# Attention in a four-phase kernel: projections at other steps, rows of maxima issued by SyncE, and an opening with buffers of its own

## The reference

```python
x = x + attention(layernorm(x))      # 4 sequences of 1024 tokens, 256 wide, 16 heads of 16, causal
x = x + moe(layernorm(x))            # one of 4 experts per token
x = x + (layernorm(x) + mamba2(layernorm(x)))
x = x + moe(layernorm(x))

def attention(x):                    # W + B A of the sequence's LoRA adapter, for Q, K, V and O
    Q, K, V = multilora(x, q), multilora(x, k), multilora(x, v)
    Q, K = rope(Q), rope(K)
    scores = where(causal, Q K^T / sqrt(16), -inf)
    return multilora(softmax(scores) V, o)
```

## Time and profile before

| | |
|---|---|
| three runs | 2194.78 us (median), 2182.81 to 2199.73 |
| the profiled execution | 2185.0 us, span 2183.1 us |
| mean granted clock of PE | 0.901 |
| busy: PE, DVE, ACT, POOL | 83%, 55%, 38%, 33% |
| DRAM read, written | 102.52 MB, 45.48 MB |

### The profile page before, as it was taken

One profiled execution on the slowest core, in us unless ns is written; L12 is line 12 of the kernel. 1 busy time (PEld: TensorE's weight loads), 2 busy tenths in 40 slices (PEclk: granted clock), 3 DMA queues, 4 the chain that ended last, 5 costly groups with the idle time before them and its releaser, 6 DMA issues. The chain is left out here.

```text
span 2183.1 us, 30159 instructions
## 1 busy us (share of the span) xinstructions
PE 1819.3 (83%) x9520; PEld 1212.1 (56%) x9520; DVE 1191.3 (55%) x2979; ACT 822.7 (38%) x1705; POOL 725.6 (33%) x922
## 2 busy tenths in 40 slices
PE   5368889889888864899999658989898938999997
PEld 3133334434433322788888535747484727888886
DVE  4466676666666508543443356665656685443442
ACT  2036655656665624111111035554646441111111
POOL 2335464464462312222222124333242312222221
PEclk9569989989988855999999969999999978999999
DMA  5522333332442108000000230100101080000000
GB/s 160 174 89 90 119 126 95 122 125 77 134 135 87 39 16 313 22 24 28 26 25 26 70 111 15 43 36 1 78 1 78 1 309 22 26 24 30 25 24 9
DMA packets 90179, 161.23 MB, mean 74 GB/s; under 512 B 23080, under 2 KB 50476, under 8 KB 88880
## 3 DMA queue, kind: packets, MB, share of 16 engines
q1 hardware_dynamic: 71504, 107.39, 14.7%
q0 software_dynamic: 17984, 50.62, 7.2%
q10 hardware_dynamic: 544, 1.31, 0.2%
HBM read 102.52 MB, written 45.48 MB: 68 GB/s over the span
## 5 line engine op out<-in xcount | busy, mean ns | idle before, releaser
L690 ACT ACTIVATE a_probs<-a_ps_e 128x512 f32<-128x512 f32 (+3 forms) x768 | 336.0, 491 | 204.1 <-PE a_ps_e L854 200.9
L438 DVE CUSTOM_DVE_ANT_0 a_ps_m<-a_ps_m,a_causal 128x512 f32<-128x512 f32 (+3 forms) x512 | 239.4, 517 | 97.5 <-PE a_ps_m L841 96.4
L1433 PE MATMUL g_ps_y<-g_w_d,x_res 128*128 x1120 | 253.2, 379 | 2.8 <-DVE x_res L1203 2.8
L854 PE MATMUL a_ps_e<-a_q_st,a_k_st 64*128 64x512 f32 (+3 forms) x768 | 187.9, 480 | 76.4 <-ACT a_probs L690 48.5
L854 PEld LDWEIGHTS a_ps_e<-a_q_st,a_k_st 64*128 64x128 f32 x768 | 79.6, 201 | 289.8 <-ACT a_probs L690 200.5
L1433 PEld LDWEIGHTS g_ps_y<-g_w_d,x_res 128*128 128x128 f32 x1120 | 212.3, 190 | 34.6 <-issue 3.2
L442 DVE TENSOR_REDUCE a_peak<-a_ps_m 128x1 f32<-128x512 f32 x256 | 164.8, 686 | 94.8 <-PE a_ps_m L841 94.1
L841 PE MATMUL a_ps_m<-a_k_st,a_q_st 64*128 64x512 f32 (+3 forms) x768 | 152.7, 399 | 68.8 <-DMA a_k_st<-a_scr_k 28.0
L1323 ACT COPY x_res<-g_ps_h 128x512 f32<-128x512 f32 x70 | 41.1, 587 | 439.2 <-PE g_ps_h L1441 439.2
L576 POOL TENSOR_SCALAR_AFFINE_SELECT a_probs<-a_probs 128x256 f32<-128x256 f32 x256 | 103.9, 408 | 284.1 <-ACT a_probs L690 283.8
L1170 DVE BATCH_NORM_STATS2 g_xe_stats<-x_res 128x6 f32<-128x256 f32 x70 | 29.9, 426 | 295.6 <-DMA x_res<-g_x_rows,g_token_i 295.6
(11 more groups left out here) (272 smaller groups left out, 3664.5 us busy)
## 6 DMA issues: line engine op xcount, KB each, us to landing
a_q_st<-a_scr_q POOLq DMA_DIRECT2D x32, 512.0 KB, 4.0
a_k_st<-a_scr_k POOLq DMA_DIRECT2D x32, 512.0 KB, 4.8
m_spread_acs<-m_acs_rows SPq DMA_DIRECT2D x8, 2048.0 KB, 9.7
a_scr_q<-a_high SPq DMA_DIRECT2D x36, 256.0 KB
a_scr_k<-a_high SPq DMA_DIRECT2D x36, 256.0 KB
a_swapped<-a_raw SPq DMA_DIRECT2D x64, 128.0 KB, 2.0
g_w_gu<-L_ffn_Wg SPq DMA_DIRECT2D x8, 1024.0 KB, 9.8
g_w_gu<-L_ffn_Wu SPq DMA_DIRECT2D x8, 1024.0 KB, 12.4
```

The lines of the kernel that those rows point to most:

```text
L438: nc.vector.tensor_tensor_reduce(ps_m[:, bank, 0:w], ps_m[:, bank, 0:w], causal[:, 512 - w:], 1.0, MASKED, ALU.add, ALU.max, peak[:, p % 2 ...
L690: nc.scalar.activation(probs[:, N % RING, r, q0:], ps_e[:, (2 * N + r) % HEAD_BANKS, q0:], ACT.Exp, scale=DH ** -0.5).then_inc(exp_done, 1)
L854: nc.tensor.matmul(ps_e[:, (2 * N + r) % HEAD_BANKS, q0:], k_st[rows(r), p % BUFS, j * P:(j + 1) * P], q_st[rows(r), p % BUFS, 512 * c + q ...
L1433: last = nc.tensor.matmul(ps_y[:, 0:D], hid_t[:, f * P:(f + 1) * P], w_d[:, bass.ds(e, 1), f].rearrange("p a d -> p (a d)"), start=(f == 0 ...
```

## The change

Six things are changed, all in the attention.

1. The projections of Q, K and of the values move from steps 3, 5, 7, 9 to steps 2, 8, 14, 20. The copies, turns, rounding and storing that follow move with them, into the next unit for parts 2 and 3. The low-rank product for the output moves from step 13 to 11.
2. `put_rows` moves from POOL to SP. ACT's copy before it writes rounded values.
3. Parts 2 and 3 of block 0 get buffers of their own (`first_high`, `first_low`, in memory of `a_probs` that is unused until the first exponentials), so ACT no longer waits for a landing before it rounds them.
4. For block 0, SP writes parts 0 and 2 and ACT writes parts 1 and 3.
5. SP loads x of sequences 1 to 3 only when pair 0 has landed.
6. The row statistics of sequence 1 are taken between chunks 22 and 42, those of sequences 2 and 3 in units 1 and 5, one tile behind a step's maxima.

```diff
-    LORA_AT, XT_AT, OUT_AT, QK_AT, V_AT, LORA_O_AT = (1, 4, 9), (6, 7, 12, 13), (15, 17, 19, 21), (3, 5, 7, 9), (3, 5, 7, 9), 13
+    LORA_AT, XT_AT, OUT_AT, QK_AT, V_AT, LORA_O_AT = (1, 4, 9), (6, 7, 12, 13), (15, 17, 19, 21), (2, 8, 14, 20), (2, 8, 14, 20), 11
...
+        def parts(blk, i):
+            if blk == 0 and i >= 2:
+                return first_high[:, i % 2], first_low[:, i % 2]
+            return high[:, i % 2], low[:, i % 2]
+
+        def keep(eng, blk, i):
+            eng.wait_ge(low_ready, 4 * blk + i + 1)
+            n, half = i % 2, i // 2
+            to = scr[n][blk % 2, :, :, :, half * 512:(half + 1) * 512]
+            hi, lo = parts(blk, i)
+            for c, part in enumerate(((hi, hi, None, lo), (hi, lo, None, hi))[n]):
+                if part is not None:
+                    eng.dma_start(to[:, c], part).then_inc(scr_out[i % 2], 16)
...
+            def put_rows(p):
+
+                sp.wait_ge(piece_act, ACT_NO["max", p] + 1)
+                for r in range(2):
+                    sp.dma_start(q_st[64 * r + 32:64 * r + 33, p % BUFS, :].bitcast(F32), less_t[r * T:(r + 1) * T, p % 2, :]).then_inc(rows_in[p % BUFS], 16)
...
-            for i in range(4):
-                keep(0, i)
+            for i in (0, 2):
+                keep(sp, 0, i)
+            sp.wait_ge(pair_in[0], 32)
             for b in range(1, BATCH):
                 sp.dma_start(X[:, b * T:(b + 1) * T], x[:, b * T:(b + 1) * T]).then_inc(x_in[b], 16)
-            for i in range(4):
+            for i in range(3):
                 swap(1, i)
-            for i in range(4):
-                keep(1, i)
+            keep(sp, 1, 0)
+            put_rows(0)
+            swap(1, 3)
+            for i in (1, 2):
+                keep(sp, 1, i)
+            put_rows(1)
+            keep(sp, 1, 3)
...
+                    for p in MAX_AT.get(U * CORE + n, []):
+                        put_rows(p)
...
-                    if g % 2 == 1 and more and n in (4, 6, 8, 11):
-                        swap(2 * b + 2 + g // 2, (4, 6, 8, 11).index(n))
-                    if g % 2 == 1 and more and n in (17, 19):
-                        keep(2 * b + 2 + g // 2, (17, 19).index(n))
-                    if g % 2 == 0 and U >= 2 and (U - 1) // GROUPS + 1 < BATCH and n in (3, 6):
-                        keep((U - 1) // GROUPS * 2 + 2 + (U - 1) % GROUPS // 2, 2 + (3, 6).index(n))
+                    if g % 2 == 1 and more and n in (3, 9, 15, 21):
+                        swap(2 * b + 2 + g // 2, (3, 9, 15, 21).index(n))
+                    if g % 2 == 1 and more and n in (14, 20):
+                        keep(sp, 2 * b + 2 + g // 2, (14, 20).index(n))
+                    if g % 2 == 0 and U >= 2 and (U - 1) // GROUPS + 1 < BATCH and n in (3, 9):
+                        keep(sp, (U - 1) // GROUPS * 2 + 2 + (U - 1) % GROUPS // 2, 2 + (3, 9).index(n))
...
-            for b in range(1, BATCH):
-                dve.wait_ge(x_in[b], 16)
-                moments(b)
-            maxima(0, CUTS[0])
+            for k in range(0, CUTS[0], 2):
+                maxima(k, k + 2)
+                if k in range(22, 22 + 2 * T, 2):
+                    row_moments(1, (k - 22) // 2)
+                if k == 42:
+                    moments(1)
...
+                    if g == 1 and b + 2 < BATCH and n in range(10, 10 + T):
+                        row_moments(b + 2, n - 10)
+                    if g == 1 and b + 2 < BATCH and n == 20:
+                        moments(b + 2)
...
-            ROPE_AT = {6: (0, 0), 7: (0, 1), 8: (0, 2), 9: (1, 0), 10: (1, 1), 11: (1, 2), 12: (2, 0), 13: (2, 1),
-                       14: (2, 2), 15: (0, 3), 17: (1, 3), 19: (3, 0), 21: (3, 1), 23: (3, 2)}
+            ROPE_AT = {5: (0, 0), 6: (0, 1), 7: (0, 2), 11: (1, 0), 12: (0, 3), 13: (1, 1), 14: (1, 2), 17: (2, 0),
+                       18: (1, 3), 19: (2, 1), 20: (2, 2), 23: (3, 0)}
+            ROPE_THEN = {0: (3, 1), 1: (2, 3), 2: (3, 2), 7: (3, 3)}
...
-                    for p in MAX_AT.get(U * CORE + n - 1, []):
-                        put_rows(p)
...
-                if blk >= 1 or i >= 2:
+                if blk >= 1:
                     act.wait_ge(scr_out[i % 2], 48 * (2 * blk + i // 2))
...
                 if e == ("v", 0, 0):
                     for i in range(4):
                         round_high(0, i)
+                    for i in (1, 3):
+                        keep(act, 0, i)
```

56 lines of the change are left out of this document (26 added, 30 removed).

## The result

The changed kernel took 2212.44 us (median of 11 runs), the kernel before 2189.49 beside it. The ratio is 1.0082, with a 95% interval of 1.0054 to 1.0110: about 18 us slower. The forecast was 2156, which is 39 us under the median of the first three runs, 2194.78. The profiled execution after took 2205.65 us, 20.65 more than the one before.

The account below looks back on a forecast made before the run. It took the opening as a chain with hardly any compute and the units as bound by PE. Opening 26 plus units 13 (rows 22, pair loads 4, even steps -13) made 39 us off 2194.78: 2156, range 2132 to 2184.

Parts of the forecast that it names:

- Opening, +26: Stretch before the units: five parts summing to 26 us gained, with bounds of 16 and 31.
- Copies: Opening, own buffers and half the copies on ACT: first load 6 us earlier; only 2 if DMA engines bind at 161 GB/s.
- x behind pair 0: Opening, x loaded only after pair 0: its loads reach PE sooner, 3 us gained, bounds 0 and 3.6.
- Statistics: Opening, row statistics moved out of DVE's way: 12 us gained, 3 lost again when sequence 1's come back between chunks.
- Second row: Opening, pair 1's maxima: shorter path from complete maxima to PE's start, 8 us gained, only 3 if copies hold ACT's rounding.
- Rows of maxima, +22: Ends of odd units: rows issued earlier by SP remove 13.7 us of waits and 8 of slow clock; bounds 10 and 31.
- The first rival: Whole kernel: exponential waits and later masks eat the rows' gain; 26 us and nothing more, about 2169; chance 0.14.
- Even steps, -13: Nine units with projections or values: pieces at even steps hide almost no exponential waits, 1.5 us lost each; bounds 0 and 16.
- Later masks: Start of a unit: a POOL turn, three operations of 1.26 us, among the first masks; taken as 0, at worst 6 us.
- The sign set for it: Profile after: the prediction is wrong if masks show as what ends PE's waits for `weigh`.
- The slower case: Units with pieces: bunching and remaining waits hold the clock low, some 10 us each, 2216 at six units; chance 0.08.
- the 0.9 that was set as a sign: Profile after: the prediction is wrong if the granted clock in units 1 to 11 falls under 0.9.

Follow-up runs that it names:

- f1: e2 with POOL's first scaling by the inverse sums moved from step 23 of odd units to step 9 of the next even unit; 2141.88 us.
- e3: The kernel before with only the rows of maxima moved from POOL to SP; 2182.18 us, 0.9938 of the kernel before.
- g4: f1 with projections and values at steps 2, 4, 6, 8 instead of 3, 5, 7, 9; 2165.15 us.
- f2: The changed kernel with the last turn behind the masks of steps 0 to 2 and the first scaling at step 9 of even units; 2179.17 us.
- g1: f2 with POOL's load of a pair in odd units at step 10 instead of 14; 2157.87 us.
- e2: The changed kernel with all pieces of the units back at their old steps, new opening and rows on SP kept; 2169.66 us.
- i1: The changed kernel with first scaling at step 9 of even units and, in odd units, SP's stores at 16 and 22, broadcast at 22; 2175.90 us.

## Why the prediction was wrong, by its own steps

**Opening, +26: right in its parts but one.** It gave 21.4 us at the second `shifted`, 23.9 at unit 1. (The recorded lower bound of 16 does not follow from the terms, whose lower ends add up to 13.5.) *Copies*: the value near the upper end was the wrong choice. The load came 1.8 us earlier, not 6; the bound from 161 GB/s had said 2. Window of the kernel after from the first store to the load:

```profile
43.44:64.60 21.16, 8.35 (x32) 6.75 (x30) 5.46 (x6) 3.29 (x6) 3.64 (x3) 0.74 0.47 161
```

The same 161 GB/s as in the earlier trace rows: two issuing engines moved the bytes no faster, and ScalarE's last three issues took 5.13 us, 1.71 each instead of 0.67. The kernel before had shown such an issue too, 1.78 us at 58.96; the 0.67 was taken from another. The rule cited in the prediction (the Trainium skill, DMA: Bandwidth & Descriptors, "Issuing engines are not separate DMA queues") pointed the right way, and the 4 us worked out by it were still too much. *x behind pair 0*: load to first chunk 5.4 us instead of 9.1, so 3.7, where 3 was taken. *Statistics*: first chunk to first reduction 0.8 us instead of 13.0, so 12.1, where 12 was taken. *Second row*, less the statistics that come back: 3.8, where 8 less 3 was taken.

**Rows of maxima, +22: wrong.** The waits for rows went as said, and the time did not come: units 1 to 12 took 506.0 us with the rows on SyncE, 505.8 without. The first rival ("only the opening pays") had named it, at 0.14, and the step that failed is its dismissal: "For it: PE is in order, and its idle time may just move. Against: the rows' waits are pure waiting and have one cause". They had one cause, and beside them stood a second wait that ended no earlier. The kernel before has it in its list of waits, 160 to 770 us, and I left it out because POOL was not the bound:

```profile
POOL a_out_t L583 <- DMA a_den<-a_inverse: 60.0, 12, 9.6
```

The total misleads as well. Seven of the twelve, 53.4 us, stand at other scalings, which cost nothing: f1 keeps 58.3 us of such waits, and no `weigh` waits there. The first scalings waited 0.6 to 2.1 us each, because POOL came to them late; in e3, with the rows early, they waited 5.1 to 5.7 us each, with the masks behind them.

**Even steps, -13: right in size, in good part by luck.** 12.1 us in g4, but priced as waits that nothing hides, of which g4 has only 2.8 us more; the other 9.3 are a lower clock, which the term did not hold.

**Later masks, 0 and "at worst 6": the step that turned the sign.** I priced the turn's three operations of 1.26 us and not what the first of them waits for. The wait is 5.34 us in unit 4, and `weigh` pays 32.0 us in six units, with matmuls at half speed behind. That is the even units' part of the loss, 24.8 us in all. The sign set for it, masks ending PE's waits for `weigh`, came true, though the list puts these waits down to "issue". Freeing the masks (changed kernel to f2) brings 33 us by medians, in the traces all of it in the even units (299.7 to 260.0). Issuing POOL's loads ahead of the waiting turns (f2 to g1) brings 21 more; in the changed kernel chunks had waited for loads only 2.3 us, in f2 14.4. Those 54 exceed the 44 of all moved steps, since g1 also rid itself of the scaling that e2 still had.

**Clock.** The slower case, at 0.08, was forecast as a clock held low by bunching in the units with pieces, 10 us in each; that its 2216 for six such units lies near 2212 is luck. The clock did fall: 0.88 in units 1 to 11, under the 0.9 that was set as a sign. In the odd units it fell for 3.5 to 10.5 us at a time, from step 10 or 11 on. In unit 3 the longest wait of TensorE ahead of that is 0.88 us. After, 262 to 274 us, steps 10 to 14 of unit 3, and then the same steps before, when no projection stood there:

```profile
262.00:265.00 3.00, 2.09 (x18) 0.78 (x16) 3.00 (x9) 2.58 (x6) 3.00 (x4) 0.99 0.16 62
265.00:274.00 9.00, 8.37 (x24) 2.87 (x24) 3.68 (x12) 4.00 (x8) 5.95 (x8) 0.50 0.47 113
```

```profile
278.45:285.75 7.30, 6.40 (x50) 2.57 (x48) 6.06 (x18) 6.74 (x15) 7.22 (x9) 1.00 0.18 64
```

The projection of step 14 falls into that stretch and takes 3.78 us instead of 1.98. I have no experiment that moves this fall by itself. Freeing the masks left the odd units as long as they were (254.8 us in the changed kernel, 259.9 in f2), so what made them 22.4 us longer stays open in the main. They got shorter with the load early (239.0 in g1), with the copies reordered (242.2 in i1) and at the old steps (226.9 in e2).

## What to carry to other kernels

Before you remove a wait, look in the same few microseconds for other engines' waits that end no earlier: they are what you will have instead. An edit to the list of an engine that works in order is priced by what each moved instruction waits for, not by how long it runs, and by all that stands behind it; keep short instructions that feed the bound engine (masks, loads, rows) ahead of anything that waits for a copy. And a copy is as late as the queue ahead of it: 128 KB needed soon go before 768 KB needed late.
